# Layer 1's position-dependent operator stored in quads of steps

## The reference

```
xu = unfold3x3(x)                            # b c h w 9
n  = sqrt(sum_c xu*xu)                       # b h w 9
op = tanh(n @ op_w.T + op_b)                 # b h w 9 9, one 9x9 operator for each pixel
x_op = einsum('bchwj,bhwjk->bchwk', xu, op)
out = einsum('bchwk,ock->bohw', x_op + xu, weight) + bias
```

## Time and profile before

| | us |
|---|---|
| median of 3 runs | 2517.36 |
| lowest, highest | 2513.78, 2520.08 |
| the profiled execution | 2509.56 |
| its span | 2507.8 |
| PE busy | 2162.4 (86%) |
| DVE busy | 1213.8 (48%) |
| ACT busy | 1153.5 (46%) |
| GpSimd busy | 185.8 (7%) |

### The profile page before, as it was taken

One profiled execution on the slowest core, in us unless ns is written; L12 is line 12 of the kernel. 1 busy time (PEld: TensorE's weight loads), 2 busy tenths in 40 slices (PEclk: granted clock), 3 DMA queues, 4 the chain that ended last, 5 costly groups with the idle time before them and its releaser, 6 DMA issues.

```text
span 2507.8 us, 85342 instructions
## 1 busy us (share of the span) xinstructions
PE 2162.4 (86%) x38916; PEld 1599.1 (64%) x38916; DVE 1213.8 (48%) x2300; ACT 1153.5 (46%) x1986; POOL 185.8 (7%) x131
## 2 busy tenths in 40 slices
PE   4778699999979999999999999999457888986754
PEld 2446244444437888988888889888355666555653
DVE  3565234444455445445445444453256776552345
ACT  0111356565655545545545545544265676741210
POOL 1000000000010000000000000000222343110000
PEclk9999899999989999999999999999677898995665
DMA  6864836767452333433333433434733555287798
GB/s 133 211 172 100 155 111 171 172 159 204 119 166 37 71 57 63 73 57 65 71 58 63 72 58 61 72 59 95 182 95 122 146 153 170 69 174 199 145 287 238
DMA packets 610284, 306.13 MB, mean 122 GB/s; under 512 B 418236, under 2 KB 586054, under 8 KB 602566
## 3 DMA queue, kind: packets, MB, share of 16 engines
q1 hardware_dynamic: 599376, 283.93, 49.1%
q10 hardware_dynamic: 10560, 16.93, 2.7%
HBM read 172.28 MB, written 128.54 MB: 120 GB/s over the span
## 4 chain that ended last, share of the span: by engine, by line
PE 76%; DVE 8%; ACT 5%; SPq 4%; issue 3%; DMA 2%; ACTq 0%; DVEq 0%
PE ps L743 20%; PE ps L680 11%; PE ps L759 10%; PE ps L718 10%; PE ps L639 9%; PE ps L687 7%; ACT arena L951 4%; PE ps L798 3%; DVE arena L1485 2%; PE ps L913 2%; DMA arena<-x_dram 1%; DVE arena L1534 1%; PE ps L880 1%; PE ps L820 1%; DVE arena L1536 1%
## 5 line engine op out<-in xcount | busy, mean ns | idle before, releaser
L743 PE MATMUL ps<-arena 62*64 62x108 f32 x11008 | 561.6, 358 | 27.2 <-DMA arena<-xcl 23.0
L1407 DVE TENSOR_TENSOR arena<-arena 128x1024 f32<-128x1024 f32 (+1 forms) x308 | 353.5, 1162 | 339.3 <-ACT arena L1025 339.2
L743 PEld LDWEIGHTS ps<-arena 62*64 62x64 f32 x11008 | 477.3, 147 | 53.5 <-DMA arena<-xcl 23.4
L1033 ACT COPY arena<-ps 128x864 f32<-128x864 f32 x258 | 226.9, 880 | 347.7 <-PE ps L759 237.0
L1025 ACT ACTIVATE arena<-ps 128x1024 f32<-128x1024 f32 (+1 forms) x308 | 295.4, 976 | 179.2 <-PE ps L718 179.0
L718 PE MATMUL ps<-arena 63*64 63x128 f32 (+1 forms) x9504 | 314.2, 271 | 13.8 <-ACT arena L1025 13.5
L951 ACT ACTIVATE arena<-arena,nmr,rstd 128x128 f32<-128x128 f32 x752 | 295.1, 512 | 33.3 <-DVE nmr L1221 33.3
L718 PEld LDWEIGHTS ps<-arena 63*64 63x64 f32 x9504 | 297.1, 138 | 18.4 <-ACT arena L1025 14.9
L680 PE MATMUL ps<-arena 128*128 128x512 f32 x640 | 288.2, 596 | 14.2 <-ACT arena L965 14.2
L759 PE MATMUL ps<-arena 64*64 64x384 f32 (+1 forms) x3168 | 260.1, 477 | 1.2 <-issue 1.2
L680 PEld LDWEIGHTS ps<-arena 128*128 128x128 f32 x640 | 120.5, 189 | 166.9 <-issue 166.9
(11 more groups left out here) (135 smaller groups left out, 1775.9 us busy)
## 6 DMA issues: line engine op xcount, KB each, us to landing
arena<-xcl SPq DMA_DIRECT2D x688, 60.0 KB, 2.6
x_dram<-arena SPq DMA_DIRECT2D x16, 2048.0 KB, 7.3
arena<-x_dram SPq DMA_DIRECT2D x16, 2048.0 KB, 15.0
arena<-l_dram SPq DMA_DIRECT2D x32, 1024.0 KB, 13.5
xcl<-arena SPq DMA_DIRECT2D x8, 3072.0 KB, 10.9
arena<-in_x SPq DMA_DIRECT2D x32, 512.0 KB, 10.1
y_dram<-arena ACTq DMA_DIRECT2D x64, 256.0 KB, 5.7
arena<-in_x SPq DMA_DIRECT2D x16, 1024.0 KB, 15.8
```

The costliest lines, as they stand in the source:

```text
L743: mm = pe.matmul(ps[T2 * j:T2 * j + T2, bank + t, STEPS * uu:STEPS * uu + STEPS], xs[T2 * t:T2 * t + C + LANES, e, j, u, :], own[T2 * t:T2 ...
L1033: nc.scalar.copy(ysb[:, :, e, u:u + UG, :].rearrange("p t u s -> p t (u s)"), ps[:, bank:bank + 2, 0:UG * STEPS]).then_inc(main_out_a, 1)
L1407: nc.vector.tensor_tensor(own, own, d, ALU.add).then_inc(op_done, 1)
```

## The change

The operator is stored in quads: four steps of a patch lie side by side (16 bytes), then the same four steps of the next patch, and so on over 128 patches; then the next four steps (2048 bytes on). `op_quads` is the whole block in that layout (27 groups, patches, 4 steps), `own_quads` a fill's part of it (two groups, one for fill 13). The main product's moving operand is now 27 runs of four values. Tanh takes the same values out of PSUM in the same order (step, then patch) and writes each 16 bytes behind the last. The addition goes over the dense stretch as before, with four values of `delta` repeated for each patch instead of one.

```
+QUAD = 4
-        def op_steps(m, f):
+        def op_quads(m):
             n = columns_of(m) * NU
-            return ops[m % 2][:, FILL * f * n:(FILL * f + 2 * fill_steps(f)) * n]
+            return ops[m % 2][:, 0:STEPS * n].rearrange("p (g x s) -> p g x s", x=n, s=QUAD)
+
+        def own_quads(m, f):
+            return op_quads(m)[:, 2 * f:2 * f + -(-fill_steps(f) // 2), :, :]
...
-                own = ops[m % 2][:, 0:STEPS * n * NU].rearrange("p (s x) -> p s x", s=STEPS)
+                own = op_quads(m)
...
-                                           own[T2 * t:T2 * t + C + LANES, :, NU * (2 * e + j) + HALF_U * (i // 8) + u], start=True, stop=True)
+                                           own[T2 * t:T2 * t + C + LANES, :, NU * (2 * e + j) + HALF_U * (i // 8) + u, :], start=True, stop=True)
...
-                nc.scalar.activation(op_steps(m, f).rearrange("p (a s x) -> p a s x", a=2, s=sub), raw_op, ACT.Tanh).then_inc(fill_tanh, 1)
+                own = own_quads(m, f).rearrange("p g x s -> p g s x") if sub == QUAD else own_quads(m, f)[:, 0].rearrange("p x (a s) -> p a s x", a=2)
+                nc.scalar.activation(own, raw_op, ACT.Tanh).then_inc(fill_tanh, 1)
...
-                own = op_steps(m, f).rearrange("p (s x) -> p s x", s=steps)
-                d = delta[:, FILL * f:FILL * f + steps].rearrange("p (s x) -> p s x", x=1).to_broadcast([P, steps, n])
+                own = own_quads(m, f)
+                d = delta[:, FILL * f:FILL * f + steps].rearrange("p (g x s) -> p g x s", x=1, s=QUAD).to_broadcast([P, steps // QUAD, n, QUAD])
```

## The result

| us | before | after |
|---|---|---|
| median | 2521.22 of 11 runs | 2530.47 of 11 runs |
| lowest, highest | 2511.70, 2529.05 | 2521.70, 2538.70 |
| ratio, 95% interval | | 1.0043, 1.0025 to 1.0061 |
| profiled execution, its span | 2509.56, 2507.8 | 2537.77, 2536.0 |

The changed kernel is 0.4% slower; the forecast was 2472, faster by 45 us. Of the 28 us between the two profiled executions, 8.0 lie ahead of layer 1's operator, where the kernels are the same (the first tanh starts at 754.75 instead of 746.78), and 8.3 behind it. From the first tanh to the end of the last mix it is 1062.4 us instead of 1050.5: 11.9 belong to the change, and the medians, 9.3 apart, are of that size. (Of the kernel before, the profiled execution was faster than all eleven runs of the table, so the 28 us overstate the difference.)

What follows compares the result with a forecast made beforehand. Layer 1 was taken as bound by PE, 47.14 us a block; afterwards ACT's queue gives 45.0. Savings of 43 + 6 + 2, less 6 lost, net 45 us: 2464 profiled, 2472 as a median, own range 2440 to 2490, overall 2395 to 2560.

Steps and rivals of the forecast that it cites:

- rival 1: Layer 1's tanh keeps its speed despite the strided write: block about 40 us, total 2367; chance 0.15 with the middle ground.
- I take twice for tanh, 1.67 ns a value: Layer 1's tanh on ACT, writing 16 bytes apart: 1.88 us against 1.02.
- pitch: Duration of a layer 1 tanh on ACT less 0.13 us hidden behind another tanh, called p: 1.75 us.
- rival 2: Layer 1's tanh write costs more than twice: about 2527 at 1.9 ns a value, 2576 at 2.08; chance 0.29.
- 24.8 + 11.5p: Time of a layer 1 block through ACT's queue and the mixes, p being tanh's pitch: 45.0 us against 47.14.
- Unlikely, since no gap reaches 2 us: Dismissal of a clock fall while PE idles between layer 1's mixes; that case was priced at 2980.
- Rival 4: The clock falls as PE idles between layer 1's mixes: block about 70 us, total 2980; chance 0.04.
- The break-even: Tanh cost in layer 1 beyond which the change loses: p = 1.94, 1.85 ns per value.

Runs made afterwards that it cites:

- Experiment 1: Changed kernel's quad reads by PE, but tanh writing densely in the old order (values in wrong places): 2389.97 us, ratio 0.9485 to the kernel before.
- Experiment 7: Three variants of the changed kernel with some PE work computed twice to fill its idle time: 2569.39, 2532.54 and 2521.46 us.
- experiment 7's first kernel: Changed kernel with eight of the fourteen fills of a block computed twice: 2569.39 us, ratio 1.0195 to the kernel before.
- experiment 7's last kernel: Changed kernel with pieces 7, 8, 12, 14, 15 and fill 8 computed twice, filling gaps ahead of both mixes: 2521.46 us, ratio 1.0006.
- experiment 3: Kernel before, with single ACT, DVE and PE operations at various distances added at its end, nothing else running: tanh written 16 bytes apart 1.96 to 2.00 us.
- experiment 4: Changed kernel's layout and result, but tanh reads PSUM 512 bytes apart and writes SBUF densely: 2396.81 us, ratio 0.9506 to the kernel before.
- experiment 8: Dense write with PSUM read 512 bytes apart, plus fills 2, 10 and 11 moved later by a piece: 2378.70 us, ratio 0.9417.
- experiment 2: Tanh writes 16 bytes apart as in the changed kernel, main product reads 512 bytes apart as before (wrong places): 2606.40 us, ratio 1.0348.

## Why the prediction was wrong

**Right: what bounded the kernel, and nearly PE's new price.** (PE is at nine tenths in slices 13 to 28, not to 29.) The forecast for a piece was 0.75 us in the chain. A piece takes 0.92 to 0.97 us in the timeline, where the end of its last matmul counts, but the work behind it starts 0.79 us after it:

```profile
1382.46 0.97 PE L748 MATMUL ps<-arena 62*64 62x108 f32 x32 [0.30 <-ACT arena L1039]
1383.25 1.93 PE L723 MATMUL ps<-arena 63*64 63x128 f32 x64
```

That agrees with runs of four alone, 8 x 100 ns; they are not quite free, as 93 ns would have been. Experiment 1 gave 2390 where rival 1 forecast 2367 for the same condition. PE's wait for the loads there, 62 us ahead of the main product instead of 23, could be the 23 us between; it was not tested by itself.

**Right: DVE's addition unchanged, and the chain through tanh and copies.** The first fills lost 8.4 us (forecast 6).

**Wrong: "I take twice for tanh, 1.67 ns a value".** This is the step that failed first: a term of the sum that was too small. Measured: 2.072 us, or (2.072 - 0.17)/1024 = 1.86 ns a value, and a pitch of 1.87 instead of 1.75. Times 11.5 tanhs a block and 20 blocks that is 28 us, and 2 in the first fills. The mechanism was the predicted one; the number is nearly that of L1062 in the earlier trace rows (1.9), which rival 2 used: "With 1.9 ns per value ... about 2527", 3 us from the median. That it came so close is partly luck: rival 2 put the pitch at 1.97 us, 0.10 too long, and what the two next paragraphs name, which it left out, made up for that. The step that failed is the choice between two ends: "twice" was taken from PE's and DVE's prices and L951's instead of from the one row of ACT that reads PSUM, as tanh does, and writes at an even distance. Where one row shares engine, source and pattern, it should weigh most.

**Wrong: "24.8 + 11.5p".** At p = 1.87 it gives 46.3 us; undisturbed blocks take 46.80, and 20 x 0.5 = 10 us. No single term is far off. In the stretch that holds these two lines (one of the chain, one of the timeline), the first copy behind the mix starts 6.14 us after the mix's start at 1375.38 (forecast 5.81 + 0.25), and the next mix 15.58 behind that copy (by the formula 15.4):

```profile
1381.52 0.89 ACT arena L1039
...
1397.10 6.01 PE L764 MATMUL ps<-arena 64*64 64x384 f32 x72
```

Copies take 912 ns on average, and up to 0.98 in the chain, instead of 880, which fits; how much of the 0.5 is theirs was not measured.

**Wrong: "Unlikely, since no gap reaches 2 us".** The clock was put at nothing in the sum, on a bound of 2 us that no row bears out. Behind the wait of 2.61 us in the earlier trace rows the kernel before does run at a granted clock of 0.50, that is 1.2 GHz (766.2 to 769.4 us), but no row said that shorter waits are harmless. The clock fell behind gaps of 0.8 to 1.2 us in eight of blocks 1 to 19, at 1.7 us each: 13.6 us in the profiled execution. Rival 4 was priced as all or nothing (2980) and so seemed absurd; it happened at the edge, for a part of one mix or of the pieces ahead of it, in every second or third block. Experiment 7 bears out the cause, idle time of PE ahead of the mix, and puts its price in the medians at about 9 us. What the chip looks at when it lowers the clock stays open: in experiment 7's first kernel PE was busier (735 us of 800) than in its last (728), and yet only there the clock fell.

**The sum.** The first tanh to the last mix was forecast 45 us shorter and came out 12 longer, 57 apart: 28 + 2 for the price of a write, 10 for the formula, 13.6 for the clock; the 3 that are left lie in blocks 20 and 21, which saved 4.6 instead of the forecast 8. The break-even that rival 2 named, 1.85 ns a value, was met almost exactly; the pitch stayed below the 1.94 that goes with it there, since tanhs behind one another hide 0.20 us each instead of 0.13. Without the clock's part the change would have made no difference, as experiment 7's last kernel is.

**Rival 1: tanh keeps its speed.** It was rightly held unlikely. In experiment 3 an output 8 bytes apart takes 1.07 us, 12 bytes 1.50, 16 bytes 2.00, 32 bytes 2.04. The Trainium skill, "SBUF — State Buffer" (Door 1: The DMA port swizzle), wants two hits in a 16-byte line for the full rate; the writes of ACT agree (two values to a line nearly free, one to a line twice as dear, and 12 bytes, four values in three lines, in between). Its addition that one can stride for free up to 4 fp32 is contradicted: four fp32 is where the full price is reached. Two hits are not enough for PE in experiment 3 either: 131 ns in runs of two, 100 in runs of four.

**Where the expected gain went.** It is all there: 131 us of PE's read (experiment 1) against 140 of ACT's write, the clock's share included. And it can be had: the same layout written densely, with tanh reading PSUM across, is 5% faster than both kernels (experiment 4), 5.8% with the fills later (experiment 8).

## What to carry to other kernels

When a layout has to be crossed between two engines, look at every place where the crossing can stand: here the same reordering cost nothing as ACT's read out of PSUM, twice the instruction as its write into SBUF, and twice the matmul as PE's read. Price a strided access by the row that shares its engine, source and distance, and run the break-even: if it lies inside the bounds, the forecast is a coin's toss. A PE that is relieved but then waits in small gaps can be granted less clock (here behind gaps of 0.8 to 1.2 us), which gives a part of the relief back.

## What was not expected of the hardware

- ACT reading PSUM 512 bytes apart is free (1.03 us alone, 1027 ns in the kernel; dense 1.02 and 1024), and reading SBUF 16 bytes apart is as dear as writing it (2.00 us; an activation of the same size from SBUF to SBUF, with neighbours side by side, takes 1.05 in the kernel before, L977).
- DVE is not alike. Copies of 128x1024, the third of each four: PSUM to SBUF densely 1.22 us, written 8 bytes apart 1.22, written 16 bytes apart and, out of SBUF, read 16 bytes apart:

```profile
2574.72 1.95 DVE L1627 COPY arena<-ps 128x1024 f32<-128x1024 f32 x1
...
2587.97 1.05 DVE L1637 COPY arena<-arena 128x1024 f32<-128x1024 f32 x1
```

  Its write 16 bytes apart pays, as ACT's does. Its read 16 bytes apart takes half of what ACT's takes (2.00 us). Whether it is free is not shown: no run has the same copy with a dense input in SBUF, and the nearest dense instruction of the kernel before, L1253 with 4096 values in 2.42 us, is faster by the value (0.59 ns against 1.03).
- Beyond 16 bytes the distance of ACT's write hardly matters: 2.00 us there, 2.04 at 32 and 1.90 at 128.
- The granted clock fell with PE at work 82% of the time (658 of 800 us) and gaps near 1 us, at a price of 1.7 us each time. In experiment 2, with waits of up to 1.1 us and PE at work 95% of the time, it did not fall in blocks 1 to 19.
